# Attention for 16 images of 32x32: one 129-column matmul for two products of P and V, a semaphore per weight tile, and new orders of issue

## What is computed

```python
h = jnp.einsum('oc,bcn->bno', wp, xf)            # wp: normalised w_proj / fan_in, 1536 x 512
q, k, v = jnp.split(h.reshape(B, N, 8, 192), 3, axis=-1)
q = pixnorm(q) * scale; k = pixnorm(k) * scale; v = pixnorm(v)
attn = softmax(jnp.einsum('bihd,bjhd->bijh', q, k), axis=2)
res = jnp.einsum('bijh,bjhd->bihd', attn, v).reshape(B, N, C)
res = jnp.einsum('oc,bnc->bon', wo, res)         # wo: normalised w_out / fan_in, 512 x 512
return (a_c * x + b_c * res) / div
```

## Time and profile before

| | us |
|---|---|
| median of 3 runs (2987.58 to 2990.43) | 2988.52 |
| the profiled execution's own time | 2986.36 |
| its span, first to last instruction | 2984.6 |
| TensorE busy (matmul) | 2933.4 (98%) |
| VectorE busy | 2581.7 (87%) |
| ScalarE busy | 2383.4 (80%) |
| GpSimd busy | 454.9 (15%) |

### The profile page before, as it was taken

One profiled execution on the slowest core, in us unless ns is written; L12 is line 12 of the kernel. 1 busy time (PEld: TensorE's weight loads), 2 busy tenths in 40 slices (PEclk: granted clock), 3 DMA queues, 4 the chain that ended last, 5 costly groups with the idle time before them and its releaser, 6 DMA issues.

```text
span 2984.6 us, 85445 instructions
## 1 busy us (share of the span) xinstructions
PE 2933.4 (98%) x36928; PEld 2013.6 (67%) x36928; DVE 2581.7 (87%) x3197; ACT 2383.4 (80%) x2993; POOL 454.9 (15%) x678
## 2 busy tenths in 40 slices
PE   7999999999999999999999999999999999999998
PEld 5776666766667667676666766667666666666765
DVE  6898888988889888898888988888888888988887
ACT  6887878878778778787787877878787787878786
POOL 0210121101211112112111111012110121101210
PEclk9999999999999999999999999999999999999999
DMA  3133414333242332333323333223323334334234
GB/s 106 41 56 63 91 36 108 51 79 79 44 97 50 81 78 48 90 62 76 72 52 85 62 79 69 65 72 62 85 63 69 76 54 96 60 63 86 40 80 103
DMA packets 459529, 211.04 MB, mean 71 GB/s; under 512 B 407952, under 2 KB 407952, under 8 KB 459152
## 3 DMA queue, kind: packets, MB, share of 16 engines
q1 hardware_dynamic: 459152, 205.58, 32.3%
HBM read 71.30 MB, written 33.55 MB: 35 GB/s over the span
## 4 chain that ended last, share of the span: by engine, by line
PE 79%; DVE 8%; POOL 5%; ACT 3%; DMA 3%; issue 2%; SPq 0%; ACTq 0%; DVEq 0%
PE ps_pv L973 21%; PE ps_score L952 19%; PE ps_dense L930 11%; PE ps_dense L932 10%; PE ps_dense L934 10%; DVE probs L780 4%; PE ps_dense L989 3%; PE ps_dense L990 2%; PE ps_dense L991 2%; DMA x_raw<-in_x 2%; POOL rs_t L442 1%; POOL rs_t L444 1%; POOL rs_t L446 1%; ACT e_tile L596 1%; DVE probs L771 1%
## 5 line engine op out<-in xcount | busy, mean ns | idle before, releaser
L780 DVE TENSOR_TENSOR probs<-e_tile,probs 128x1024 f16<-128x1024 f32 x1024 | 1241.4, 1230 | 64.6 <-ACT probs L603 58.7
L596 ACT ACTIVATE e_tile<-ps_score,shift 128x1024 f32<-128x1024 f32 x1024 | 1107.9, 1118 | 223.7 <-PE ps_score L952 130.2
L973 PEld LDWEIGHTS ps_pv<-v_pair,probs 128*128 128x128 f16 x24576 | 772.2, 98 | 183.5 <-issue 112.4
L973 PE MATMUL ps_pv<-v_pair,probs 128*128 128x65 f16 (+1 forms) x24576 | 821.6, 193 | 2.9 <-DVE probs L780 1.7
L952 PE MATMUL ps_score<-qkT 64*128 64x512 f16 x6144 | 753.4, 378 | 3.3 <-ACT e_tile L596 3.1
L930 PE MATMUL ps_dense<-wpT_hi,x_hi 128*128 128x512 f32 x1536 | 621.0, 404 | 2.4 <-DVE wpT_lo L851 2.3
L932 PE MATMUL ps_dense<-wpT_lo,x_hi 128*128 128x512 f32 x1536 | 600.1, 391 | 0.0
L934 PE MATMUL ps_dense<-wpT_hi,x_lo 128*128 128x512 f32 x1536 | 599.0, 390 | 0.0
L603 ACT ACTIVATE probs<-e_tile 128x1024 f16<-128x1024 f32 x512 | 542.8, 1061 | 22.8 <-PE ps_pv L973 4.0
L952 PEld LDWEIGHTS ps_score<-qkT 64*128 64x128 f16 x6144 | 257.0, 94 | 361.4 <-issue 90.2
L771 DVE CAST probs<-e_tile 128x1024 f16<-128x1024 f32 x512 | 360.0, 703 | 72.0 <-PE ps_pv L973 67.6
(11 more groups left out here) (50 smaller groups left out, 1739.4 us busy)
## 6 DMA issues: line engine op xcount, KB each, us to landing
x_raw<-in_x SPq DMA_DIRECT2D x128, 256.0 KB, 3.4
x_res<-in_x SPq DMA_DIRECT2D x128, 256.0 KB, 3.6
out<-x_res SPq DMA_DIRECT2D x128, 256.0 KB, 2.5
arena<-in_w_proj SPq DMA_DIRECT2D x24, 128.0 KB, 2.9
qkT<-arena SPq DMA_TRANSPOSE x128, 4.8
resT<-res_split SPq DMA_TRANSPOSE x128, 3.6
arena<-in_w_out SPq DMA_DIRECT2D x1, 1024.0 KB, 8.0
```

What stands on the lines that cost most here:

```text
L596: act.activation(e_tile[:, t % E_BUFS, :, :], ps_score[:, t % 2, :, :], ACT.Exp, bias=shift[:, 0:1], scale=1.0 / (QK_UP * QK_UP)).then_inc ...
L780: dve.tensor_tensor(probs_of(b, t, 1), e_tile[:, t % E_BUFS, :, :], probs_of(b, t, 0), ALU.subtract).then_inc(probs_low, 1)
L973: mm = pe.matmul(ps_pv[:, h, o:o + n], probs_of(b, t, part)[:, h, queries], v[:, cols], start=(j == 0 and it == 0 and part == 0 and cols.s ...
```

## The change

- In `v_pair` the low values now lie at columns 0 to 63, the high values at 64 to 127, the ones at 128. For query tiles 1, 2 and 3 a single matmul of 129 columns multiplies the high probabilities by low values, high values and ones, into 129 columns of `ps_pv`; the low probabilities by high values and ones (65 columns) add to the upper 65 of them. Query tile 0 keeps the three matmuls into 65 columns, because 4 x 129 columns don't fit a bank of 512. A slot has 18 matmuls in place of 24.
- `take_pv` has to add the two parts: a reciprocal of 8 elements per partition, a multiplication of the high parts of 3 tiles (384 elements), one of their low parts (384), one of tile 0 (128), after which `pv_taken` lets TensorE go on, and an addition (384), after which `high_res` may start. Before: the reciprocal and one multiplication of 512 elements.
- Each tile of w_proj has its own semaphore and its own place in the SP order.
- New tables STEADY, FIRST, LAST, with other bank choices.

```diff
-        LOW = D + 8
+        HIGH = D
+        BOTH = HIGH + SUMS
+        QUERIES = 4
...
+        res_low_part = sb("res_low_part", [P, 2, QUERIES - 1, D], F32)
...
-        w_loaded = [sem(f"w_loaded{g}") for g in range(W_GROUPS)]
+        w_loaded = [sem(f"w_loaded{m}") for m in range(WP_TILES + 1)]
...
-                act.wait_ge(pv_taken, UNITS * b + u + 1)
+                act.wait_ge(res_made, UNITS * b + u + 1)
...
-                act.wait_ge(w_loaded[m // 4], 16 * (8 if m < WP_TILES else 1))
+                act.wait_ge(w_loaded[min(m, WP_TILES)], 16 * (2 if m < WP_TILES else 1))
...
-                sums = ps_pv[:, :, 0:4 * SUMS].rearrange("p h (i c) -> p h i c", c=SUMS)
-                dve.reciprocal(inv_sum[:, u % 2, :, :], sums[:, :, :, D]).then_inc(pv_inverted, 1)
+                inv = inv_sum[:, u % 2, :, :]
+                dve.reciprocal(inv, ps_pv[:, :, D:D + BOTH * (QUERIES - 1) + 1:BOTH]).then_inc(pv_inverted, 1)
 
                 after(dve, res_low, done - 1)
+                made = res[:, u % 2, :, :].rearrange("p i (h d) -> p h i d", d=D)
+                parts = ps_pv[:, :, SUMS:SUMS + BOTH * (QUERIES - 1)].rearrange("p h (i c) -> p h i c", c=BOTH)
+                whole = inv.unsqueeze(3).broadcast_to([P, 2, QUERIES, D])
                 dve.wait_ge(pv_inverted, done + 1)
-                dve.tensor_tensor(res[:, u % 2, :, :].rearrange("p i (h d) -> p h i d", d=D),
-                                  sums[:, :, :, 0:D],
-                                  inv_sum[:, u % 2, :, :].unsqueeze(3).broadcast_to([P, 2, 4, D]),
+                dve.tensor_tensor(made[:, :, 1:, :], parts[:, :, :, HIGH:HIGH + D], whole[:, :, 1:, :],
+                                  ALU.mult).then_inc(pv_scaled, 1)
+                dve.tensor_tensor(res_low_part[:, :, :, :], parts[:, :, :, 0:D], whole[:, :, 1:, :],
+                                  ALU.mult).then_inc(pv_scaled, 1)
+                dve.tensor_tensor(made[:, :, 0, :], ps_pv[:, :, 0:D], whole[:, :, 0, :],
                                   ALU.mult).then_inc(pv_taken, 1)
+                dve.wait_ge(pv_scaled, 2 * done + 2)
+                dve.tensor_tensor(made[:, :, 1:, :], made[:, :, 1:, :], res_low_part[:, :, :, :],
+                                  ALU.add).then_inc(res_made, 1)
...
-                        for it in range(4):
+                        high, low, both = slice(HIGH, HIGH + SUMS), slice(0, D), slice(0, BOTH)
+                        for it in range(QUERIES):
                             queries = slice(it * P, (it + 1) * P)
-                            o = it * SUMS
-                            for part, cols in ((0, slice(0, SUMS)), (0, slice(LOW, LOW + D)), (1, slice(0, SUMS))):
+                            o = it * BOTH
+                            products = ((0, high, o), (0, low, o), (1, high, o)) if it == 0 else                                        ((0, both, o - HIGH), (1, high, o))
+                            for part, cols, at_col in products:
                                 n = cols.stop - cols.start
-                                mm = pe.matmul(ps_pv[:, h, o:o + n], probs_of(b, t, part)[:, h, queries], v[:, cols],
-                                               start=(j == 0 and it == 0 and part == 0 and cols.start == 0),
+                                mm = pe.matmul(ps_pv[:, h, at_col:at_col + n], probs_of(b, t, part)[:, h, queries],
+                                               v[:, cols], start=(j == 0 and it == 0 and part == 0 and cols is high),
                                                stop=(j == UNIT_SLOTS - 1), skip_group_check=True)
```

More of the change, by code:

```diff
@@ new lines @@
+    "TURN_QK_AT": (13584, 32928, 46080, 48592, 49392, 51120, 51600, 51616),
+    "HIGH_QK_AT": (-14880, -6496, 14272, 17216, 17280, 19104, 29648, 31712),
+    "LOW_QK_AT": (-3584, 96, 15696, 16768, 17200, 22256, 37216, 38384),
+    "TAKE_AT": (6720, 20896, 26176, 37664, 44800, 56224, 61968, 66656),
+    "TURN_RES_AT": (49424, 51568, 51584, 52368, 52736, 98448, 98496, 114144),
+    "HIGH_RES_AT": (15328, 22048, 31296, 40912, 42096, 50704, 52016, 70800),
+    "LOW_RES_AT": (16448, 23296, 38400, 44816, 54592, 62224, 63328, 81200),
@@ new lines @@
+    "STORE_AT": (98944, 111328, 114192, 114240, 116448, 116512, 118896, 119664),
+    "W_LOAD_AT": (12992, 13040, 13056, 13072, 13088, 13120, 13152, 13168, 13184, 13200, 13232, 13264, 13280),
+    "W_SQUARE_AT": (15424, 15472, 15488, 15504, 15520, 15552, 15568, 15664, 15680, 15728, 15760, 15776, 15840,
+        15872, 15936, 15984),
+    "W_HIGH_AT": (15600, 15616, 15632, 15648, 15952, 16000, 16080, 16096, 16176, 16192, 16224, 16256, 16272,
+        16336, 16352, 16384),
+    "W_NORM_AT": (15120, 15296, 15520),
@@ L275 @@
+    "STORE_AT": (54176, 54192, 54256, 54288, 54320, 54336, 54384, 54400),
+    "PROJ_BANK": (0, 1, 0, 1, 0, 1, 0, 1, 0, 1, 0, 1, 0, 1, 0, 0, 1, 1, 0, 0, 1, 0, 0, 1),
     "OUT_BANK": (0, 1, 0, 1, 0, 1, 0, 1),
@@ L506, in turn_res, with load_weights @@
                              transpose=True).then_inc(res_turned[half], 16)
-            def load_weights(g):
-                if 4 * g >= WP_TILES:
-                    sp.dma_start(w_raw[:, 4 * g:4 * g + 4, :], wo_in).then_inc(w_loaded[g], 16)
+            def load_weights(m):
+                if m == WP_TILES:
+                    sp.dma_start(w_raw[:, WP_TILES:, :], wo_in).then_inc(w_loaded[m], 16)
                     return
-                for i in range(GROUP_UNITS):
-                    p, kind = LAYOUT[GROUP_UNITS * g + i]
-                    for h in range(2):
-                        sp.dma_start(w_raw[h * D:(h + 1) * D, 4 * g + i, :],
-                                     wp_in[2 * p + h, WEIGHT_ROWS[kind], :, :]).then_inc(w_loaded[g], 16)
+                p, kind = LAYOUT[m]
+                for h in range(2):
+                    sp.dma_start(w_raw[h * D:(h + 1) * D, m, :],
+                                 wp_in[2 * p + h, WEIGHT_ROWS[kind], :, :]).then_inc(w_loaded[m], 16)
             names = dict(load_x="LOAD_X_AT",
@@ L528, in task @@
             def task(b, s, when):
-                for g in when["w_load"].get(s, ()):
-                    load_weights(g)
+                for m in when["w_load"].get(s, ()):
+                    load_weights(m)
                 for piece in when["load_x"].get(s, ()):
@@ L574, in high_v @@
                 heads = slice(2 * (p % 2), 2 * (p % 2) + 2)
-                act.activation(v_pair[:, heads, half * HALF_NT:(half + 1) * HALF_NT, 0:D]
+                act.activation(v_pair[:, heads, half * HALF_NT:(half + 1) * HALF_NT, HIGH:HIGH + D]
                                .rearrange("p h n d -> p n h d"),
```

240 lines of the change are left out of this document (113 added, 127 removed), and 72 rows, old and new, of tables (FIRST, LAST, STEADY).

## The result

The changed kernel took 2980.41 us (median; 2978.82 to 2982.26), the kernel before, run beside it, 2988.66 us (2987.12 to 2990.43). The ratio is 0.9972, 95% interval 0.9963 to 0.9982. That is 8 us faster; the forecast was 26 us faster, and the time lies inside the forecast range. The profiled execution of the changed kernel has a span of 2978.4 us, against 2984.6 before.

The account below looks back on a forecast made before the run. TensorE's instruction stream bounds the steady images, VectorE the last image. From 2986.4: -29 (matmuls) -3 (start) -1 (A4) +2 (steady) +3 (first) +2 (last) = -26, so 2960.4; expected median 2962.5 us, range 2941 to 2984.

Parts of the forecast that it names:

- the sum over the tightest stretch: Slots 44 to 47 of a steady image: VectorE needs 6.7 us, TensorE 7.3, so 0.6 us of slack remains.
- the account of the banks: Output projection's 18 us of waits behind ScalarE's copy: whether the new order brings like waits; 0 with 15 us either way.
- the attention matmuls: Attend calls on TensorE: 12 of 48 matmuls fewer save 57 ns per call, 29 us in all, bounds 21.5 and 43.
- The rival of a larger gain: Attention matmuls: loads were the brake, the high bound holds, 14 us more gain, 2948 us; chance 0.2.
- Wide matmuls slower than pairs: Rival in attention: a wide matmul waits out its 98 ns load, 37 ns more each, about 3220 us; chance 0.02.
- The take: VectorE's take grows from 0.91 to 1.96 us, 134 us of VectorE's time over 128 units, covered on average by idle time.
- The steady images: Longer take hidden in VectorE's 22.7 us of idle time per image; 0.1 us per image for misses, 2 us.
- VectorE as the pacemaker: Slower rival: VectorE sets the steady images' pace, price up to 134 us, 3014 us at two fifths exposed; chance 0.08.
- The rival of no difference: Matmuls save only 21.5 us and fuller VectorE gives 20 back in waits for `probs`; about 2988 us; chance 0.1.
- The last image: VectorE is full there; 3 takes cost up to 1.05 us each, against O1 starting before A31; 2 us lost.
- The start and the first image: Earlier norm brings the first projection near 20 us, 3 us gained; about 3 exposed takes in the first image cost 3 us.
- The take's release: TensorE's first attend of the next unit (A4): more work lies before it, removing perhaps 1 us of waits on pv_taken.

Follow-up runs that it names:

- new order, old arithmetic: Changed kernel's tables, banks and weight loads with the old matmuls (64 and 65 columns apart) and the old short take; 2981.16 us, ratio 0.9978 to the kernel before.
- wide matmul undone: Changed kernel with each 129-column matmul split into one of 64 and one of 65, longer take, order and loads kept; 2992.03 us, ratio 1.0014.
- bank mended: Changed kernel with the last two output banks of image 14 exchanged (0 and 1 in place of 1 and 0); 2972.47 us, ratio 0.9948.
- bank mended, short take: Bank mended, without multiplication and addition of the low values for three of four query tiles (not the whole product); 2957.69 us, ratio 0.9891.
- bank mended, longer take: Bank mended, with the low product written a second time into an unread tile before the bank's release; 2994.84 us, ratio 1.0017.

## Why the prediction was right in direction and wrong in size

The forecast was a gain of 26 us, the measured one is 8. Three steps failed: the sum over the tightest stretch, which put the longer take at 2 us in the steady images (it costs 5 to 10); the account of the banks, put at 0 (the new order wins 19 us in the steady images and one bank loses 8.5 us in the last image); and the price of the attention matmuls, where 57 ns saved per call were forecast and 40 measured. That the time still falls into the forecast range is partly luck, since the 19 us won were not foreseen and pay for most of what was missed. Spans in the trace by stretch, in us (first projection to first scores of the second image; from there to the first scores of the last image; from there to the last scores; the rest):

| kernel | first image | 14 steady images | last image | rest |
|---|---|---|---|---|
| before | 207.0 | 2570.3 | 150.9 | 33.6 |
| new order, old arithmetic | 208.1 | 2551.2 | 164.1 | 36.4 |
| wide matmul undone | 211.4 | 2556.3 | 167.5 | 35.7 |
| changed | 210.5 | 2548.1 | 165.3 | 34.7 |
| bank mended | 210.5 | 2547.7 | 156.7 | 34.7 |
| bank mended, short take | 208.0 | 2537.6 | 154.5 | 34.8 |
| bank mended, longer take | 213.8 | 2564.3 | 160.8 | 34.7 |

The forecast, with 29/16 = 1.8 us of matmuls for each image, was -3 for the start, 3 - 1.8 = +1.2 for the first image, -25.4 - 1 + 2 = -24.4 for the steady ones and 2 - 1.8 = +0.2 for the last. Measured are -2.9, +3.5, -22.2 and +15.5. So the largest part of the miss lies in the last image, and the steady images come out near the forecast by errors that cancel.

- **The attention matmuls** (29 us, bounds 21.5 and 43): measured 40 ns per call, 20.5 us, at the low bound and a little below it. The starts of matmuls in the trace say why: most narrow ones are followed by the next at 29 ns, and about every fifth one 7 ns later (4424 such late starts in fourteen images before, 3622 after: 0.82 of them, where the matmuls fell to 0.75). After a wide one the next starts at 56 ns, and about every third time at 62 ns: 1881 of the late starts stand there. The forecast had taken a wide matmul at 56.1 ns without late starts and kept the narrow ones as measured; what it missed is that late starts come behind wide matmuls too. This term is 8.5 us of the miss. Why late starts occur, no run shows. The rival of a larger gain fell with it.
- **Wide matmuls slower than pairs** didn't happen: 36 matmuls, 12 of them wide, take 1.51 us, and a wide one 56 or 62 ns from start to start. The Trainium skill, "TensorE: Matmul & The Clock Gate", Back-to-back issue gap, has about 81 ns for a matmul of 128 columns in such a stream; the trace doesn't agree, as before.
- **The take** was right, 1.91 us against 1.96, and so was VectorE's total (122.6 us more, forecast some 130).
- **The steady images.** The forecast took 181.5 us an image and "the steady images at no cost for this, with 0.1 us per image for small misses"; measured are 182.0 (the addition L819 stands at 1338.12 us and, an image later, at 1520.16 us). That the sum nearly fits hides errors that cancel. The order alone wins 19.1 us in the steady images (2570.3 - 2551.2), about the 18 us of waits behind ScalarE's copy that it took away, where I had put 0 with 15 either way. With the short take the new matmuls win 13.6 us more there (2551.2 - 2537.6), where I had put 25.4; of their 18 us in the chain some 4 don't arrive. And the longer take costs 5.1 us beside narrow matmuls (2556.3 - 2551.2) and 10.1 us beside wide ones (2547.7 - 2537.6), where I had put 2. The step that failed is the sum over the tightest stretch: 6.7 us of VectorE against 7.3 of TensorE. The place was right, and TensorE does wait there, at slot 47. But the durations came from an undisturbed stretch, and this one has GpSimd's norm beside it. VectorE in the changed kernel, at that place in order of time, and then 4 us behind the norm in the chain of waits (start, us until the next):

```profile
1469.71 0.78 DVE L775 CAST probs<-e_tile 128x1024 f16<-128x1024 f32 x1
1470.41 1.34 DVE L784 TENSOR_TENSOR probs<-e_tile,probs 128x1024 f16<-128x1024 f32 x1
1471.67 0.78 DVE L812 TENSOR_TENSOR res_split<-res,res_split 128x512 f16<-128x512 f32 x1
```
```profile
1481.62 0.68 DVE probs L775
1482.31 1.13 DVE probs L784
```

  From start to start a cast takes 0.70 us and a low part 1.26 us there, where the sum had 0.60 and 1.13. With these, 3 x 0.70 + 4 x 1.26 + 0.4 = 7.5 us, more than TensorE's 7.3, and the slack of 0.6 us is gone. Beyond that, one tight place was the wrong thing to look for. The stretch of full VectorE is 54 us long, it holds three takes, and a mend at one point of it only moves the wait. The sign named for this, waits for L784 of tens of us, didn't show (6.3 us), though VectorE took back most of the gain: it was seen only by comparing runs and chains.
- **VectorE as the pacemaker** (chance 0.08) came true for a stretch, though not for the image: the longer take costs 10.9 us beside narrow matmuls and 14.8 beside wide ones, far from the 52 us of the rival's price. The rival of no difference described this mechanism rightly but looked for it at L784 alone.
- **The last image** (2 us): 14.4 us from its first scores to its last (165.3 after, 150.9 before). The sign that the forecast had named for being wrong here, new waits for a bank, did show. The step that failed is the account of the banks: it looked at the steady images, where P0 S15 A13 P1 P2 S16 stand between O5 and O6, and not at the last one, which has no next projection and whose table puts nothing else between the two. With the bank mended it is 8.5 us shorter (165.29 against 156.75), which is the bank's share; with the old arithmetic on top 155.3, so 4.4 us belong to the new order of the last image and only some 1.4 to the new arithmetic. The takes alone, short against long, are 2.2 us there, as the forecast had it.
- **The start and the first image** (-3 and +3): the start is right, -2.9 us. The takes cost 2.5 us in the first image (210.5 - 208.0), near the 3; but the image as a whole is 3.5 us longer, where with its share of the matmuls 1.2 were forecast.
- **The take's release** (-1): wrong in sign. The 17 waits of 7.5 us are those of the loads. Of the matmuls only one waited for the take before:

```profile
PE ps_pv L973 <- DVE res L792: 0.3, 1, 0.3
```

  After, three matmuls wait 3.7 us for it, one in the first image and two in the last; in the steady images none does, before or after. The forecast had looked at the orders of the steady images alone.

## What to carry to other kernels

An engine at 90% busy isn't one with 10% to spare: look for its long stretches without a gap, and price what is added there higher than what is added beside gaps. The length of such a stretch is no price by itself: in the old order the new arithmetic lengthens VectorE's longest one from 26 to 36 us only, less than the 54 us in the new order, and yet it costs 34 us there, with 68 waits of TensorE for the low probabilities. A change of order and a change of arithmetic that come together want to be timed apart; here the order did all of it, and the arithmetic pays, by 3 us, only in the units where VectorE has room. When an order is written out by hand for a steady state, the last but one round is a case of its own, since the work that stood between two uses of a buffer can be missing from it.

## What was not expected of the hardware

VectorE is slower while GpSimd works. In the changed kernel, VectorE's groups from 1463 to 1478 us, with the norm beside them, and then from 1478 to 1503 us, without:

```profile
L784 DVE TENSOR_TENSOR probs<-e_tile,probs 128x1024 f16<-128x1024 f32 x8 | 10.2, 1287 | 0.0
L775 DVE CAST probs<-e_tile 128x1024 f16<-128x1024 f32 x4 | 3.1, 764 | 0.2 <-PE ps_pv L987 0.2
```
```profile
L784 DVE TENSOR_TENSOR probs<-e_tile,probs 128x1024 f16<-128x1024 f32 x11 | 13.1, 1216 | 0.1
L775 DVE CAST probs<-e_tile 128x1024 f16<-128x1024 f32 x5 | 3.4, 682 | 0.0
```

That is 6% for the subtraction and 12% for the cast on average, and single ones reach 1.34 and 0.78 us. It holds over the whole trace: the 776 subtractions with no GpSimd instruction beside them take 1217 ns on average and none over 1.23 us, the 233 wholly beside such instructions 1292 ns. GpSimd's instructions are small there (128 x 64 elements). What they share, the rows don't say.
